# Attention kernel: the weighing of the values by a block's probabilities in one piece, in the first of four steps, in place of two halves two steps apart

## The chip, the cores and the metric

The kernel runs on one core of one Trainium2 chip. The metric is the device time of one execution in microseconds (us). The names of the engines are those of the profile: PE is TensorE's matmul, PEld its loading of weights, DVE is VectorE, ACT is ScalarE, POOL is GpSimd and SP is SyncE, which here issues the DMAs.

## The reference

Two residual layers follow one another on x of shape (4, 32, 32, 384). The first is a selective scan in four directions and is not touched here. The second is attention over the 1024 tokens of an image with 12 heads of 32 channels:

```python
qkv = (x.reshape(B, L, dim) @ w_qkv + b_qkv).reshape(B, L, 3, nh, hd)
q, k = rot(q), rot(k)
attn = jnp.einsum('bnqd,bnkd->bnqk', q, k) * scale
attn = attn.reshape(B, nh, H, W, H, W) + rel_h[..., :, None] + rel_w[..., None, :]
attn = jax.nn.softmax(attn.reshape(B, nh, L, L), axis=-1)
out = jnp.einsum('bnqk,bnkd->bnqd', attn, v)
...
return out @ w_proj + b_proj
```

The change concerns the second einsum, the sum over the keys of probability times value.

## The kernel before

**Stages.** The scan of the four images takes the first 1,700 us or so; nothing of it is touched. Then the four images go through attention one after the other. An image has three groups of four heads (`GROUPS` is 3, `HG` is 4), a group has eight blocks of 128 queries (`QB` is 8). One head of one block is a step: 32 steps in a group (`STEPS`), 96 in an image. Block n of an image has the steps 4n to 4n + 3.

**What is done for a step s.** TensorE makes the scores of 128 queries against 1024 keys (`scores`, line 880, two matmuls of 64 rows by 512 columns). VectorE adds the bias and takes the largest (`biased_scores`, line 1201), ScalarE takes the exponential (line 1526), TensorE turns the 128 by 1024 probabilities in eight transposes (`turn_probs`, line 891), and the turned ones are copied from PSUM to `PT`: by VectorE for even s (line 1155), by ScalarE for odd s (line 1503); both functions are called `save_turned`. When all four heads of a block are turned and saved, TensorE weighs the values with them (`weigh`, line 905): 32 matmuls, eight tiles of keys times four heads, each with 128 rows, 32 output channels and 128 queries. The four heads write into four parts of one PSUM region. ScalarE copies the sum out (`save_sums`, line 1509).

**Order on each engine.** Nothing here is placed by a scheduler: each engine's queue is written out and holds the steps in this order.

- TensorE at step s: `scores(s + 2)`, then a job if the step has one, then a piece of `weigh` if s is odd, then `turn_probs(s)`. `scores(s)` waits until the turned probabilities of step s - 4 are saved, since both use the same PSUM banks. `turn_probs(s)` waits for the exponential of s and for the largest of s + 1.
- VectorE at step s: if s is odd `save_turned(s - 3)`, then `biased_scores(s)`, then its part of a job.
- ScalarE at step s: if s is even `save_turned(s - 3)`, in one step of four `save_sums`, then the exponential of s, then its part of a job.

**Jobs.** A table `JOB_AT` puts other work into some steps. In group 0 nearly every even step has one (k = 2, 4, 6, 8, 10, 12, 16, 18, 20, 22, 24 and 26, and also 25 and 27): first projections of the next groups' q and k (line 561, three matmuls), then products with the tables of relative positions (lines 854 and 843). Group 1 has two projections, at k = 6 and 10. In group 2 the table `LATE_AT` has sums, normalizations and output projections at k = 2, 4, 6, 8, 10, 12, 20, 22, 24, 26 and 28 (lines 925, 934 and 561). All other steps hold attention alone.

**Change of group.** The operands of the next group's head j are brought by six DMAs (line 542), which SP issues once `scores` of step 32g - 4 + j has been done. `scores(32g + j)` waits for them.

**Weighing before.** In each block n but the last of an image, the two calls `weigh(n, 0)` and `weigh(n, 1)`, of 16 matmuls each, stand in steps 4n + 5 and 4n + 7. The last block is weighed in one call behind the loop.

Of the kernel before, what the change touches and what calls it, by code (L numbers as in the profile page):

```python
# [19 lines left out]
HG = P // HD  # L20
# [121 lines left out]
def build(nc, x, mats, cols, sel_in, onehot, b_rows, z_rows, x1, xn2, out):  # L142
    ctx = ExitStack()
    with ctx:
# [30 lines left out]
        def banks(k, n=2):  # L175
            return PS[:, k * HALF:(k + n) * HALF]
# [380 lines left out]
        def _(pe):  # L557
# [222 lines left out]
            for b in range(B):  # L780
                for i in range(ITEMS):
                    s, n = divmod(i, NST)
# [21 lines left out]
            for b in range(B):  # L804
# [58 lines left out]
                def wait_turned_saved(s):  # L863

                    pe.wait_ge(pt_saved[s % 2].sem, pt_saved[s % 2].after(b, s // 2 + 1))

                def scores(s):
                    g, k = divmod(s, STEPS)
                    qb, j = divmod(k, HG)
                    if qb == 0:  # L870
                        pe.wait_ge(head_loaded[j].sem, head_loaded[j].after(b, HEAD_DMAS * (g + 1)))
                    if s == 1:
                        pe.wait_ge(rel_saved.sem, rel_saved.after(b, 2))
                    elif s == 3:
                        pe.wait_ge(max_done.sem, max_done.after(b, 2))
                    elif s >= 4:
                        wait_turned_saved(s - 4)
                    for h in range(2):
                        rows = slice(2 * HD * h, 2 * HD * h + 2 * HD)
                        last = pe.matmul(scores_place(s)[:, h * HALF:(h + 1) * HALF],  # L880
                                         QX[rows, j, qb * P:(qb + 1) * P], KX[rows, j, :], start=True, stop=True)
                    last.then_inc(s_psum.sem, 1)

                def turn_probs(s):
                    pe.wait_ge(exp_done.sem, exp_done.after(b, s + 1))
                    if s + 1 < STEPS * GROUPS:
                        pe.wait_ge(max_done.sem, max_done.after(b, s + 2))
                    else:
                        wait_turned_saved(s - 3)
                    for t in range(QB):  # L890
                        last = pe.transpose(turned_place(s)[:, t * P:(t + 1) * P], PR[s % 3][:, t * P:(t + 1) * P], idn)  # L891
                    last.then_inc(pt_psum.sem, 1)

                def weigh(n, part, parts=2):

                    g = n // QB
                    if part == 0:
                        for s in (HG * n + HG - 2, HG * n + HG - 1):
                            wait_turned_saved(s)
                        if n:  # L900
                            pe.wait_ge(o_saved.sem, o_saved.after(b, n))
                    for t in range(part * QB // parts, (part + 1) * QB // parts):
                        for j in range(HG):
                            head = HG * g + j
                            last = pe.matmul(banks(6, 1)[HD * j:HD * j + HD, (n % 2) * P:(n % 2 + 1) * P],  # L905
                                             V[:, t, head * HD:(head + 1) * HD], PT[:, n % 2, j, t, :],
                                             start=(t == 0), stop=(t == QB - 1), skip_group_check=True)
                    if part == parts - 1:
                        last.then_inc(o_psum.sem, 1)
# [36 lines left out]
                def project(m, ks):  # L946
                    for k in ks:
                        last = pe.matmul(banks(m, 1), W["w_proj"][:, k, m * P:(m + 1) * P], OT[:, k, HALF:L],  # L948
                                         start=(k == 0), stop=(k == CT - 1), skip_group_check=True)
                    return last  # L950
# [11 lines left out]
                for s in range(STEPS * GROUPS):  # L962
                    g, k = divmod(s, STEPS)
                    if s + 2 < STEPS * GROUPS:
                        scores(s + 2)
                    if k in JOB_AT[g]:
                        job(g + 1, JOB_AT[g][k])
                    if g + 1 == GROUPS and k in LATE_AT:
                        late(LATE_AT[k])
                    if s % 2 == 1 and s > HG:  # L970
                        weigh((s - HG - 1) // HG, (s - HG - 1) % HG // 2)
                    if s + 1 == STEPS * GROUPS:
                        wait_turned_saved(s - 2)
                        project(0, (0, 1))
                        project(1, (0, 1))
                    turn_probs(s)
# [793 lines left out]
```

## Time and profile before

| what | value |
|---|---|
| median of 3 runs | 3094.75 us (3092.77 to 3095.74) |
| profiled execution | 3094.16 us |
| its span in the trace | 3092.4 us |
| PE busy | 2684.6 us, 87% of the span |
| DVE busy | 2242.5 us, 73% |
| ACT busy | 1614.7 us, 52% |
| POOL busy | 1351.2 us, 44% |
| mean granted TensorE clock | 0.968 of full speed |

A row of a timeline gives the start in us from the start of the span, the duration of the row, the engine, the line and operation, what it writes and reads, and how many instructions follow one another in it. A float32 matmul has two records, so the two matmuls of `scores` are x4 and 16 matmuls of `weigh` are x32. In brackets stands how long the engine was idle before it and who ended that. The ends of matmuls are modelled, so distances between the starts of two rows are the safer measure of TensorE.

### The profile page before, as it was taken

Reading aid. Unit: us, or ns where it says so; the run is one execution under the profiler, and the core shown is the slowest. Engines: PE = TensorE matmul, PEld = TensorE weight load, DVE = VectorE, ACT = ScalarE, POOL = GpSimd, SP = SyncE. Lnnn points to the kernel's source line nnn. Section 1 sums busy time; section 2 is a strip of 40 time slices with the busy share of each in tenths; the row PEclk is TensorE's granted clock in tenths of the full one; section 3 lists DMA queues with packets and bytes.
Section 4 is the critical chain, followed back from the end, with each engine's and each line's share of the span. In section 5 each row is a group of like instructions: output and inputs, shape, how many; then the busy total and the mean of one; then the engine's idle time right before and its main releaser. Section 6 shows DMA issues by size and latency. Waiting matters only on the chain. (4 is left out here: it accounts for less than half of the span.)

```text
span 3092.4 us, 40835 instructions
## 1 busy us (share of the span) xinstructions
PE 2684.6 (87%) x16088; PEld 1346.6 (44%) x16088; DVE 2242.5 (73%) x2157; ACT 1614.7 (52%) x1972; POOL 1351.2 (44%) x624
## 2 busy tenths in 40 slices
PE   5579788988889878687767999999999999999999
PEld 2134233333333333232322565555555565556555
DVE  0398988899888998899992566646665566646665
ACT  2464655555555556555541456625564356525564
POOL 1577887887778877788670200011000300011000
PEclk9799999999999999999996999999999999999999
DMA  2344544455444555445551210120120210120110
GB/s 78 108 142 129 163 150 144 150 140 168 165 145 148 142 170 167 154 160 140 197 172 36 76 36 18 39 75 1 36 56 14 63 36 22 35 76 1 35 36 22
DMA packets 93526, 297.03 MB, mean 96 GB/s; under 512 B 16172, under 2 KB 18872, under 8 KB 93208
## 3 DMA queue, kind: packets, MB, share of 16 engines
q1 hardware_dynamic: 93336, 294.43, 30.8%
q8 instruction: 128, 2.10, 0.3%
q14 instruction: 62, 0.51, 0.1%
HBM read 238.27 MB, written 23.07 MB: 85 GB/s over the span
## 5 line engine op out<-in xcount | busy, mean ns | idle before, releaser
L1599 POOL TENSOR_TENSOR arena<-arena 128x1024 f32<-128x1024 f32 x384 | 903.2, 2357 | 307.4 <-DVE arena L1081 297.7
L1081 DVE TENSOR_TENSOR_SCAN arena<-PS,arena 128x1024 f32<-128x1024 f32 x384 | 879.0, 2289 | 102.2 <-ACT PS L1442 70.9
L577 PE MATMUL PS<-arena,ident 128*128 128x512 f32 x1536 | 762.0, 620 | 15.0 <-ACT arena L1453 12.8
L1442 ACT ACTIVATE PS<-arena,a_inf,a_neg 128x1024 f32<-128x1024 f32 x384 | 463.8, 1208 | 586.3 <-DVE arena L1081 580.3
L1201 DVE CUSTOM_DVE_ANT_1 arena<-PS,arena 128x1024 f32<-128x1024 f32 x384 | 467.7, 1219 | 323.4 <-PE PS L880 321.8
L1526 ACT ACTIVATE arena<-arena,neg_max 128x1024 f32<-128x1024 f32 x384 | 441.0, 1148 | 494.8 <-DVE neg_max L1201 494.8
L1089 DVE TENSOR_TENSOR arena<-arena,PS 128x1024 f32<-128x1024 f32 x384 | 460.8, 1200 | 57.7 <-PE PS L568 56.4
L568 PE MATMUL PS<-arena,sel 96*128 96x512 bf16 x768 | 239.4, 394 | 295.5 <-DVE arena L1089 291.7
L1629 POOL TENSOR_TENSOR arena<-arena 128x512 f32<-128x512 f32 x48 | 68.4, 1425 | 955.2 <-ACT arena L1495 955.2
L880 PE MATMUL PS<-arena 64*128 64x512 f32 x1536 | 431.6, 640 | 19.3 <-DMA arena<-arena 12.8
L577 PEld LDWEIGHTS PS<-arena,ident 128*128 128x128 f32 x1536 | 302.5, 198 | 275.0 <-issue 221.4
L891 PE MATMUL PS<-ident,arena 128*128 128x128 f32 x3072 | 414.7, 278 | 3.8 <-ACT arena L1526 3.6
L891 PEld LDWEIGHTS PS<-ident,arena 128*128 128x128 f32 x3072 | 334.9, 142 | 154.9 <-issue 92.5
L568 PEld LDWEIGHTS PS<-arena,sel 96*128 96x128 bf16 x768 | 55.9, 100 | 577.5 <-DVE arena L1089 503.3
L1155 DVE COPY arena<-PS 128x1024 f32<-128x1024 f32 x192 | 233.9, 1218 | 60.6 <-PE PS L891 57.2
L905 PEld LDWEIGHTS PS<-arena 128*32 128x32 f32 x6144 | 157.0, 110 | 134.0 <-issue 131.7
L905 PE MATMUL PS<-arena 128*32 128x128 f32 x6144 | 206.5, 276 | 0.0
L1503 ACT ACTIVATE arena<-PS 128x1024 f32<-128x1024 f32 x192 | 192.7, 1004 | 19.4 <-PE PS L891 19.4
L880 PEld LDWEIGHTS PS<-arena 64*128 64x128 f32 x1536 | 116.5, 185 | 88.5 <-issue 59.0
L1636 POOL TENSOR_TENSOR arena<-arena 128x512 f32<-128x512 f32 x48 | 64.0, 1333 | 176.3 <-DVE arena L1126 175.7
L561 PE MATMUL PS<-normed,arena 128*128 128x512 f32 x288 | 135.7, 615 | 0.6 <-DVE g_tmp L1025 0.6
L577 PE MATMUL PS<-arena 128*128 128x512 f32 (+1 forms) x224 | 108.3, 622 | 12.0 <-ACT arena L1305 5.5
(125 smaller groups left out, 2205.3 us busy)
## 6 DMA issues: line engine op xcount, KB each, us to landing
arena<-b_rows SPq DMA_DIRECT2D x256, 512.0 KB, 3.7
arena<-b_rows SPq DMA_DIRECT2D x256, 256.0 KB, 3.9
arena<-arena SPq DMA_DIRECT2D x192, 128.0 KB, 3.3
arena<-arena SPq DMA_DIRECT2D x120, 64.0 KB, 2.6
normed<-x_in SPq DMA_DIRECT2D x12, 512.0 KB, 5.4
residual<-x_in SPq DMA_DIRECT2D x12, 512.0 KB, 5.6
x<-residual SPq DMA_DIRECT2D x12, 512.0 KB, 5.3
xn<-residual SPq DMA_DIRECT2D x12, 512.0 KB, 4.7
```

The source lines that it names most:

```text
L568: last = pe.matmul(dst[:, half(h)], lhs, rhs(h), start=(k == 0), stop=(k == len(pairs) - 1))
L577: last = pe.matmul(dst[:, half(h)], lhs, rhs[:, half(h)], start=start, stop=stop, skip_group_check=True)
L880: last = pe.matmul(scores_place(s)[:, h * HALF:(h + 1) * HALF], QX[rows, j, qb * P:(qb + 1) * P], KX[rows, j, :], start=True, stop=True)
L891: last = pe.transpose(turned_place(s)[:, t * P:(t + 1) * P], PR[s % 3][:, t * P:(t + 1) * P], idn)
L905: last = pe.matmul(banks(6, 1)[HD * j:HD * j + HD, (n % 2) * P:(n % 2 + 1) * P], V[:, t, head * HD:(head + 1) * HD], PT[:, n % 2, j, t, :] ...
L1081: dve.tensor_tensor_scan(HS[:, at % 2, ::step], DA[:, ::step], DBU[:, at % R3, ::step], 0.0, ALU.mult, ALU.add).then_inc(scan_done.sem, 1)
L1089: dve.tensor_tensor(HC[:, at % R_HC, :], HS[:, at % 2, :], C_PSUM, ALU.mult).then_inc(hc_ready.sem, 1)
L1155: dve.tensor_copy(PT[:, n % 2, s % HG, :, :], turned_place(s).rearrange("p (t q) -> p t q", t=QB)).then_inc(pt_saved[0].sem, 1)
L1201: dve.tensor_tensor_reduce(out=PR[s % 3].rearrange("p (h w) -> p h w", w=IMG), in0=scores_place(s).rearrange("p (h w) -> p h w", w=IMG), i ...
L1442: act.activation(DA, DELTA[:, tile % 2, :], ACT.Exp, bias=a_inf[:, col:col + 1], scale=a_neg[:, col:col + 1]).then_inc(da_ready.sem, 1)
L1526: act.activation(PR[s % 3], PR[s % 3], ACT.Exp, bias=neg_max[:, s % 4:s % 4 + 1], scale=-1.0, accum_out=row_sum[:, qb, at:at + 1]).then_in ...
L1599: pool.tensor_tensor(DBU[:, at % R3, :], DU[:, tile % 2, :], BSB[:, at % R3, :], ALU.mult).then_inc(dbu_ready.sem, 1)
```

## The change

`weigh` is called once for a block, in step 4n + 5, with all 32 matmuls. The step 4n + 7 has no piece of it any more. The 32 matmuls and their order within the block are the same, and no other engine's queue changes.

```diff
@@ -967,8 +967,8 @@
                         job(g + 1, JOB_AT[g][k])
                     if g + 1 == GROUPS and k in LATE_AT:
                         late(LATE_AT[k])
-                    if s % 2 == 1 and s > HG:
-                        weigh((s - HG - 1) // HG, (s - HG - 1) % HG // 2)
+                    if s % HG == 1 and s > HG:
+                        weigh(s // HG - 1, 0, 1)
                     if s + 1 == STEPS * GROUPS:
                         wait_turned_saved(s - 2)
                         project(0, (0, 1))
```

TensorE's queue in group 1 behind its last job, before. L880 is `scores`, L905 `weigh`, L891 `turn_probs`; here a matmul counts once.

```order
1165 L880 MATMUL PS<-arena 128x512 x2
1166 L905 MATMUL PS<-arena 32x128 x16
1167 L891 MATMUL PS<-ident,arena 128x128 x8
1168 L880 MATMUL PS<-arena 128x512 x2
1169 L891 MATMUL PS<-ident,arena 128x128 x8
1170 L880 MATMUL PS<-arena 128x512 x2
1171 L905 MATMUL PS<-arena 32x128 x16
1172 L891 MATMUL PS<-ident,arena 128x128 x8
1173 L880 MATMUL PS<-arena 128x512 x2
1174 L891 MATMUL PS<-ident,arena 128x128 x8
```

The same four steps in the changed kernel:

```order
1155 L880 MATMUL PS<-arena 128x512 x2
1156 L905 MATMUL PS<-arena 32x128 x32
1157 L891 MATMUL PS<-ident,arena 128x128 x8
1158 L880 MATMUL PS<-arena 128x512 x2
1159 L891 MATMUL PS<-ident,arena 128x128 x8
1160 L880 MATMUL PS<-arena 128x512 x2
1161 L891 MATMUL PS<-ident,arena 128x128 x8
1162 L880 MATMUL PS<-arena 128x512 x2
1163 L891 MATMUL PS<-ident,arena 128x128 x8
```

Four steps held two pieces of 16 in alternate steps; now one step holds 32, and three steps in a row hold scores and transposes alone.

TensorE's queue at the end of an image, before. L948 is the output projection.

```order
1296 L880 MATMUL PS<-arena 128x512 x2
1297 L905 MATMUL PS<-arena 32x128 x16
1298 L891 MATMUL PS<-ident,arena 128x128 x16
1299 L905 MATMUL PS<-arena 32x128 x16
1300 L948 MATMUL PS<-arena 128x512 x4
1301 L891 MATMUL PS<-ident,arena 128x128 x8
```

And in the changed kernel:

```order
1274 L880 MATMUL PS<-arena 128x512 x2
1275 L905 MATMUL PS<-arena 32x128 x32
1276 L891 MATMUL PS<-ident,arena 128x128 x16
1277 L948 MATMUL PS<-arena 128x512 x4
1278 L891 MATMUL PS<-ident,arena 128x128 x8
```

The 16 matmuls that stood between the transposes and the output projection now stand ahead of the transposes.

## Rows read from the trace of the kernel before

**Rows 1.** The page, busy time, share of the span and instructions of each engine.

```profile
PE 2684.6 (87%) x16088; PEld 1346.6 (44%) x16088; DVE 2242.5 (73%) x2157; ACT 1614.7 (52%) x1972; POOL 1351.2 (44%) x624
```

**Rows 2.** Windows: busy us (instructions) by engine, granted clock, DMA share, GB/s.

```profile
2197.13:2288.60 91.47, 88.36 (x910) 52.42 (x910) 59.23 (x86) 56.47 (x91) 5.09 (x4) 1.00 0.16 34
2083.66:2394.30 310.64, 303.90 (x2992) 180.19 (x2993) 200.28 (x292) 172.01 (x272) 20.13 (x16) 1.00 0.11 27
```

**Rows 3.** Timeline of TensorE over two steps in group 1 without a job.

```profile
2205.40 1.13 PE L880 MATMUL PS<-arena 64*128 64x512 f32 x4
2206.46 1.09 PE L891 MATMUL PS<-ident,arena 128*128 128x128 f32 x8
2207.48 1.13 PE L880 MATMUL PS<-arena 64*128 64x512 f32 x4
2208.54 1.08 PE L905 MATMUL PS<-arena 128*32 128x128 f32 x32
2209.55 1.09 PE L891 MATMUL PS<-ident,arena 128*128 128x128 f32 x8
```

**Rows 4.** Timeline of TensorE where a product of the same shape precedes `weigh`.

```profile
2173.63 1.08 PE L843 MATMUL PS<-arena 128*32 128x128 f32 x32
2174.53 1.06 PE L905 MATMUL PS<-arena 128*32 128x128 f32 x32
2175.52 1.09 PE L891 MATMUL PS<-ident,arena 128*128 128x128 f32 x8
```

**Rows 5.** Timeline of all engines, group 1, from one `scores` on.

```profile
2200.23 1.13 PE L880 MATMUL PS<-arena 64*128 64x512 f32 x4
...
2201.40 1.22 DVE L1201 CUSTOM_DVE_ANT_1 arena<-PS,arena 128x1024 f32<-128x1024 f32 x1 [1.86 <-PE PS L880]
...
2202.55 1.22 DVE L1155 COPY arena<-PS 128x1024 f32<-128x1024 f32 x1
...
2203.69 1.21 DVE L1201 CUSTOM_DVE_ANT_1 arena<-PS,arena 128x1024 f32<-128x1024 f32 x1
...
2204.94 1.15 ACT L1526 ACTIVATE arena<-arena,neg_max 128x1024 f32<-128x1024 f32 x1 [1.03 <-DVE neg_max L1201]
...
2206.09 1.00 ACT L1503 ACTIVATE arena<-PS 128x1024 f32<-128x1024 f32 x1
```

**Rows 6.** Timeline at the one wait in an image of `scores` for ScalarE's copy.

```profile
2238.75 1.00 ACT L1503 ACTIVATE arena<-PS 128x1024 f32<-128x1024 f32 x1
...
2239.81 1.13 PE L880 MATMUL PS<-arena 64*128 64x512 f32 x4 [1.03 <-ACT arena L1503]
```

**Rows 7.** Timeline in group 0, step 16: VectorE's copy and `scores(18)`, which waits for it.

```profile
2140.14 1.22 DVE L1155 COPY arena<-PS 128x1024 f32<-128x1024 f32 x1
...
2141.45 1.13 PE L880 MATMUL PS<-arena 64*128 64x512 f32 x4
```

**Rows 8.** Timeline of SP and TensorE at the two changes of group of one image.

```profile
2177.77 16.00 SPq L542 DMA_DIRECT2D arena<-arena  x24
...
2197.13 1.13 PE L880 MATMUL PS<-arena 64*128 64x512 f32 x4 [1.03 <-DMA arena<-arena]
...
2288.55 1.13 PE L880 MATMUL PS<-arena 64*128 64x512 f32 x4 [0.80 <-DMA arena<-arena]
```

**Rows 9.** Timeline in group 1 with a projection in step 38 (the scores start 1.06 earlier).

```profile
2211.64 2.84 PE L561 MATMUL PS<-normed,arena 128*128 128x512 f32 x6
...
2215.28 1.13 PE L880 MATMUL PS<-arena 64*128 64x512 f32 x4
...
2218.94 1.00 ACT L1503 ACTIVATE arena<-PS 128x1024 f32<-128x1024 f32 x1
```

**Rows 10.** Timeline at the end of an image: ScalarE's copy of step 93, then the projection.

```profile
2032.61 1.00 ACT L1503 ACTIVATE arena<-PS 128x1024 f32<-128x1024 f32 x1
...
2033.93 3.70 PE L948 MATMUL PS<-arena 128*128 128x512 f32 x8
```

## The prediction, made before the changed kernel ran

> **What bounds the kernel now.** I read the page first: TensorE is busy for 87% of the span, VectorE for 73%, ScalarE for 52% [rows 1]. Such shares average over stages, so the second view is the windows over one image of attention: of 310.64 us TensorE is busy for 303.90, VectorE for 200.28, ScalarE for 172.01 [rows 2]. Attention is bound by TensorE with 2% of idle, and the four images do the same, so each term below is worked out for one image and taken four times. What remains to be asked is how much slack the other engines have, since the change leaves TensorE's work alone and only moves it. That is read from the timeline, from start to start.
>
> On TensorE scores take 1.06 us until the transposes start, the transposes 1.02 until the next scores, and a piece of 16 weighing matmuls adds 1.01 (2208.54 to 2209.55) [rows 3]. So a bare step takes 2.08, a step with a piece 3.09.
>
> Beside it runs a chain over the other engines, which starts with `scores(36)` at 2200.23: largest on VectorE at 2201.40, VectorE's copy at 2202.55, the next largest at 2203.69, its exponential on ScalarE at 2204.94, ScalarE's copy at 2206.09 [rows 5]. That copy frees the banks for `scores(39)`. How long after its start the scores can go is seen where they do wait for it: 2238.75 to 2239.81, 1.06 us [rows 6]. So the chain from `scores(36)` until `scores(39)` may start is 2206.09 + 1.06 - 2200.23 = 6.92 us. TensorE needs for the same way (steps 34, 35 and 36: bare, with a piece, bare) 2207.48 - 2200.23 = 7.25 [rows 3, 5]. The slack is 0.33 us: this is the number on which the change turns.
>
> **The change, first part: the block in one piece.** Between `weigh` and the transposes TensorE needs more than between two rows of `weigh`'s own shape: 16 matmuls take 0.90 when 16 of the same shape follow, and 0.99 to 1.01 when the transposes follow [rows 3, 4]. So 32 in a row take 0.90 + 0.99 = 1.89 in place of 2 x 1.01 = 2.02: 0.13 gained a block. Of 23 blocks of an image one gains nothing, that of steps 25 and 27: there a product of the same shape stands ahead of both pieces already (before 2 x 1.89 = 3.78; afterwards 0.90 + 1.89 and 1.01, 3.80). Gain: 22 x 0.13 = 2.86 us an image.
>
> A rule bears on this. The Trainium skill, TensorEngine Tiling (Array Packing), section Key Properties, says that "Changing tiling mode (not just tile) drains the TensorE". The 0.90 against 1.01 agrees. By that rule alone the change removes a pair of mode changes a block and is a gain; that is the first rival below.
>
> **Second part: three bare steps in a row.** The steps 4n + 2, 4n + 3 and 4n + 4 now hold scores and transposes alone, so TensorE comes from `scores(4n + 4)` to `scores(4n + 7)` in 3 x 2.08 = 6.24 us. The chain still takes 6.92; it starts anew at each `scores`, since VectorE was idle for 1.86 before it [rows 5]. TensorE waits 6.92 - 6.24 = **0.68 us**, and the weighing of step 4n + 5 is queued behind the waiting scores. The heavy step cannot give this back: its 32 matmuls come after the wait, and the time that they leave to the others is not needed. The other waits of a bare step hold: VectorE's copy starts 2.32 after `scores(36)` and takes 1.22 [rows 5], so it ends at 3.54, and the scores of an even step that need it start at 4.16. What `weigh` waits for was saved before its scores started, and ScalarE's short `save_sums` is over within the 1.06 of the scores.
>
> There are 22 such places in an image (n = 1 to 22); what differs is what else is in the three steps:
>
> - Five in group 1 (`scores` 39, 51, 55, 59, 63) and one in group 2 (83) are bare: 6 x 0.68 = 4.08.
> - Two in group 1 (43, 47) have a projection in the first of the three steps. It delays the copies as well as TensorE. The chain from the scores at 2210.58 ends at 2218.94 + 1.06 = 2220.00, 9.42; TensorE needs 2215.28 - 2210.58 = 4.70 and two bare steps, 8.86 [rows 9]. Wait 0.56 each: 1.12.
> - Two in group 2 (75, 87) have four short transposes of sums in the last step, which cover part. Between 0 and 0.68 each; I take half, 0.68 for both.
> - Ten have a longer job in the second or third step: six in group 0 (11 to 31) and four in group 2 (71, 79, 91, 95). A projection adds 4.70 - 2.08 = 2.62 [rows 9] and VectorE's part of an earlier one adds less to the chain. Nothing.
> - Two fall on the change of group (35, 67), next.
>
> **Third part: waits that exist already and grow.** (a) `scores(18)` in group 0 starts at 2141.45; VectorE's copy before it, delayed by two operations of a job, runs from 2140.14 to 2141.36 [rows 7], so the scores could start at 2141.42. Step 15 loses its piece, TensorE is there at 2140.44: a wait of 0.98. (b) At the first change of group the path is set by SP, whose 24 DMAs are issued from 2177.77 for 16.00 us, and `scores(35)` waits 1.03 [rows 8]. Whatever TensorE saves in the steps 26 to 32 is waited for: one piece, 1.01. (c) At the second, where it waits 0.80 already [rows 8], it saves 3 x 1.01 - 1.89 = 1.14, of which the wait of `scores(63)` has taken 0.68: 0.46 more. (d) At the end of an image the projection starts at 2033.93 and needs ScalarE's copy of step 93, which allows 2032.61 + 1.06 = 2033.67 [rows 10]. Now the transposes of 93 come 0.88 later, behind 32 matmuls, and the copy goes to about 2033.00 and allows 2034.06, while TensorE is ready at 2033.80: 0.26.
>
> **A wait that goes:** the 1.03 of `scores(49)` [rows 6]. `scores(47)` now waits 0.56 itself and the heavy step 45 follows, so TensorE arrives later than the copy.
>
> **Sum for one image.** Waits: 4.08 + 1.12 + 0.68 + 0.98 + 1.01 + 0.46 + 0.26 - 1.03 = 7.56. Gain: 2.86. Net 4.70, for four images 18.8 us. Against the profiled execution's own time: 3094.16 + 18.8 = 3113.0. The median is 0.6 above that execution, which I leave out: **3113 us**, 0.6% slower. If each length in the chain is off by 0.02, a wait is off by about 0.1, for a dozen waits in four images 5 us; the two half-covered places are good for 2.7 either way. The forecast's own range is 3105 to 3121.
>
> **Rivals.**
>
> 1. *The gain of the block alone, no wait: faster.* The step that decides is the copy on ScalarE; if it came 0.68 us sooner than in the rows, the three bare steps would be free and 4 x 2.86 = 11.4 us would be gained: 3083. For it speaks that ScalarE and VectorE are idle for a third of the image and more [rows 2]. Against it: their idle time lies before the chain starts, not in it; its five parts follow one another within 0.1 us [rows 5].
> 2. *The waits, but no gain.* The 0.90 is measured with another line's matmuls ahead [rows 4]; if 32 of `weigh`'s take 2.02, the sum is 4 x 7.56 = 30.2: 3124.
> 3. *The bare steps do not wait, only the special places do.* Then 0.98 + 1.01 + 1.14 + 0.26 - 1.03 - 2.86 = -0.50 an image, 3092, no change. It needs the same early copy as rival 1, with the change of group still set by SP.
> 4. *The clock falls.* Ten short waits an image could cost granted clock. In the stretch with waits of 1.03 and 0.80 and more the granted clock is 1.00, the 2.4 GHz level [rows 2]. If a bare step of 2.08 ran at 1.2 GHz after each of the 40 waits, it would cost 40 x 2.08 = 83 us: 3196. The Trainium skill, TensorE: Matmul & The Clock Gate, section "A second HAM failure mode: psum-queue depth-cycling", describes such a case, a TensorE that "micro-idles between MM groups" and changes between its clock levels; the waits in this trace do not bear it out.
>
> That the change does nothing is excluded: the order of the queue shows 32 matmuls in one row and a step without them.
>
> **How the numbers follow.** Forecast 0.77; rival 1 0.05, rival 2 0.08, rival 3 0.07, rival 4 0.03. A measurement of this kernel tells about 0.2% (6 us) from no change, so faster means below 3088.6 (rival 1), within it rival 3 and a little of the forecast's lower edge, slower the rest: 0.05, 0.08, 0.87. The range leaves out rivals 1, 3 and 4 (0.15), reaches from somewhat below the forecast's own range to rival 2: 3101 to 3125.
>
> **What would show it.** In the changed kernel's waits, `scores` (line 880) should wait for ScalarE's copy (line 1503) about 10 times an image, some 24 us in all, in place of 4 times and 4.1 us; the rows of `weigh` should read x64 with 1.89 until the transposes; the waits of `scores` for the DMAs should be 1.01 and 0.46 longer; VectorE's and ScalarE's busy times should be the same. If `scores(51)` starts without a wait, the chain is wrong; if 32 matmuls take 2.0, the gain is; if group 0 loses more than 1 us an image, the cover by jobs is.

## The result, and the profile of the changed kernel

The changed kernel takes 3111.76 us (median of 6 runs, 3107.41 to 3113.68), the kernel before 3094.6 us beside it. The ratio is 1.0055, with a 95% interval of 1.0043 to 1.0067: slower by 17 us. Forecast were 3113 us in a range of 3101 to 3125, and slower. The profiled execution took 3110.13 us, 15.97 more than the one before.

The waits of TensorE's matmuls in the attention stage of the changed kernel (engine, line and tile, who ended the wait, us in total, times, longest):

```profile
PE PS L880 <- ACT arena L1503: 20.4, 40, 0.6
PE PS L880 <- DMA arena<-arena: 15.8, 13, 1.9
PE PS L948 <- DVE arena L1172: 6.8, 4, 1.7
PE PS L880 <- DVE arena L1155: 3.6, 4, 0.9
...
PE PS L948 <- ACT arena L1503: 1.0, 4, 0.2
```

There are 40 waits of `scores` for ScalarE's copy, ten in each image, where before there was one of 1.03 [rows 6]. New, too, are four for VectorE's copy (`scores(18)`) and four of the projection at the end of an image. The wait of L948 for L1172 was there before, of the same length. So were waits of `scores` for the DMAs; the line of the kernel before is:

```profile
PE PS L880 <- DMA arena<-arena: 12.8, 12, 1.7
```

They grew by 3.0 us in the four images, where the prediction's 1.01 and 0.46 an image make 5.9. This is the one sign of the prediction that came out at half its size; the cause is in the point on the first change of group below.

The timeline in group 1 of the second image, from one `scores` to the one that waits:

```profile
2243.01 1.13 PE L880 MATMUL PS<-arena 64*128 64x512 f32 x4
2244.07 1.09 PE L891 MATMUL PS<-ident,arena 128*128 128x128 f32 x8
2244.19 1.22 DVE L1201 CUSTOM_DVE_ANT_1 arena<-PS,arena 128x1024 f32<-128x1024 f32 x1 [1.55 <-PE PS L880]
2245.10 1.13 PE L880 MATMUL PS<-arena 64*128 64x512 f32 x4
2245.34 0.08 DVE L1201 DVE_READ_ACCUMULATOR2_ANT neg_max<- 128x1 f32 x1
2245.34 1.22 DVE L1155 COPY arena<-PS 128x1024 f32<-128x1024 f32 x1
...
2246.48 1.21 DVE L1201 CUSTOM_DVE_ANT_1 arena<-PS,arena 128x1024 f32<-128x1024 f32 x1
...
2247.18 1.13 PE L880 MATMUL PS<-arena 64*128 64x512 f32 x4
...
2247.73 1.15 ACT L1526 ACTIVATE arena<-arena,neg_max 128x1024 f32<-128x1024 f32 x1 [1.03 <-DVE neg_max L1201]
2248.24 1.09 PE L891 MATMUL PS<-ident,arena 128*128 128x128 f32 x8
...
2248.88 1.00 ACT L1503 ACTIVATE arena<-PS 128x1024 f32<-128x1024 f32 x1
...
2249.93 1.13 PE L880 MATMUL PS<-arena 64*128 64x512 f32 x4 [0.60 <-ACT arena L1503]
```

This is the chain of [rows 5], with the same distances: from the scores at 2243.01 to the copy's start at 2248.88, and 1.05 later, at 2249.93, the scores go: 6.92 us. TensorE's last transposes started at 2248.24, so it was ready at 2248.24 + 1.02 = 2249.26 and lost 0.67. The row's own figure, 0.60, counts from the modelled end of the transposes.

TensorE over the next four steps:

```profile
2249.93 1.13 PE L880 MATMUL PS<-arena 64*128 64x512 f32 x4 [0.60 <-ACT arena L1503]
2250.99 1.95 PE L905 MATMUL PS<-arena 128*32 128x128 f32 x64
2252.88 1.09 PE L891 MATMUL PS<-ident,arena 128*128 128x128 f32 x8
2253.90 1.13 PE L880 MATMUL PS<-arena 64*128 64x512 f32 x4
...
2260.83 1.13 PE L880 MATMUL PS<-arena 64*128 64x512 f32 x4 [0.61 <-ACT arena L1503]
```

The whole block takes 2252.88 - 2250.99 = 1.89 us, as forecast from [rows 4]. A period of four steps takes 2260.83 - 2249.93 = 10.90; before it was twice 2.08 + 3.09, 10.34. The difference, 0.56, is within 0.02 the wait less the gain of the block, 0.67 - 0.13.

Where the 15.97 us are, by the starts of `scores` (L880), mean of the four images in us:

| from scores to scores | before | changed | difference |
|---|---|---|---|
| 0 to 28 (group 0) | 92.88 | 94.02 | +1.14 |
| 28 to 35 (first change of group) | 20.76 | 20.06 | -0.70 |
| 35 to 60 (group 1) | 71.65 | 74.70 | +3.05 |
| 60 to 67 (second change of group) | 19.79 | 19.65 | -0.14 |
| 67 to 95 (group 2) | 86.73 | 87.09 | +0.37 |

That is 3.72 an image, 14.9 for four. Attention began 0.44 later, and 0.6 lie behind `scores(95)`, in the stretches to the next image or to the end. In three images the stretch in group 1 took 74.30; in the fourth it took 75.91, of which more at the end.

### The profile page after: what moved, and what is told of

It is laid out like the page before. It is cut to its first block and busy times, and to the rows that moved or that the text cites. A ratio compares the mean times of both kernels' runs of the same rounds, so it can differ in the third digit from the quotient of the medians.

```text
span 3108.3 us, 40835 instructions
## 1 busy us (share of the span) xinstructions
PE 2674.9 (86%) x16088; PEld 1350.4 (43%) x16088; DVE 2243.9 (72%) x2157; ACT 1616.2 (52%) x1972; POOL 1352.2 (44%) x624
## 5 line engine op out<-in xcount | busy, mean ns | idle before, releaser
L880 PE MATMUL PS<-arena 64*128 64x512 f32 x1536 | 432.1, 641 | 42.1 <-ACT arena L1503 20.4
L891 PEld LDWEIGHTS PS<-ident,arena 128*128 128x128 f32 x3072 | 334.7, 141 | 200.9 <-issue 170.3
L891 PE MATMUL PS<-ident,arena 128*128 128x128 f32 x3072 | 414.8, 278 | 2.7 <-ACT arena L1526 2.7
L905 PEld LDWEIGHTS PS<-arena 128*32 128x32 f32 x6144 | 163.3, 110 | 70.3 <-issue 51.1
L905 PE MATMUL PS<-arena 128*32 128x128 f32 x6144 | 188.8, 275 | 0.0
L880 PEld LDWEIGHTS PS<-arena 64*128 64x128 f32 x1536 | 116.1, 184 | 114.9 <-issue 53.6
```

## The experiments

The theory: three bare steps in a row take 6.24 us and the chain to ScalarE's copy 6.92, so the scores wait; and the changes of group are set by SP's DMAs. The times of the kernel before lay between 3093.6 and 3094.6 us beside each set of runs.

**ScalarE's copy one place earlier, in the changed kernel.**

```diff
-                    if s % 2 == 0 and s > 3:
-                        save_turned(s - 3)
+                    if s % 2 == 1 and s > 2:
+                        save_turned(s - 2)
...
-                save_turned(STEPS * GROUPS - 3)
                 save_sums(QB * GROUPS - 2)
```

> The changed kernel with one more edit: ScalarE copies the turned probabilities of the odd step s - 2 ahead of the exponential of step s (s odd), in place of those of s - 3 ahead of the exponential of s + 1. The same instructions, one place earlier in ScalarE's queue. My theory (the chain over VectorE and ScalarE's exponential to ScalarE's copy takes 6.92 us where three bare steps take 6.24): the copy can run as soon as the transposes are done, the 10 waits of scores for it in an image (0.60 us each in the changed kernel's trace) vanish, and the time falls by about 4 x 5.0 = 20 us from the changed kernel's to about 3 us below the kernel before (3089 to 3094). Part of what is gained in groups 0 and 1 is waited for again at the change of group: the wait of scores(66) and (67) for the DMAs grows to about 3.8 us an image. Rival 'the waits come from TensorE itself or from PSUM, not from the copy's place in the queue': the time stays at 3108 to 3114, with waits of the same number. Rival 'everything is gained': 4 x 2.86 = 11.4 us below the kernel before plus the 4.1 us of its own waits, 3079.

Measured: 3089.91 us (3086.18 to 3097.81), ratio to before 0.9991 (0.9982 to 0.9999), 22 us less than the changed kernel in medians, 20 by the two ratios to the kernel before. Its waits:

```profile
PE PS L880 <- DMA arena<-arena: 19.9, 13, 1.9
PE PS L948 <- DVE arena L1172: 6.8, 4, 1.7
PE PS L880 <- DVE arena L1155: 3.6, 4, 0.9
```

All 40 waits of scores for ScalarE's copy are gone, with the same instructions on every engine. So the place of the copy in ScalarE's queue, behind the exponential of s + 2, is what the bare steps waited for. Part of the gain was eaten by the DMAs, as expected, though less than expected: all waits for them rose from 15.8 to 19.9 us, and by the rows those of `scores(66)` and `(67)` from 2.4 to 3.0 us an image, where 3.8 was expected.

**The same edit in the kernel before.**

> The kernel before with ScalarE's copy one place earlier, as in the run on the changed kernel, the weighing in two halves. My theory: with halves two steps apart the copy has 0.33 us of slack already, so only the one wait of an image for it (1.03 us, scores(49)) goes: 4 us less than the kernel before (about 3090). Rival 'the early copy is a gain of its own in every step': 10 us or more below.

Measured: 3089.6 us, ratio 0.9987 (0.9978 to 0.9996), 4 us less, as the one wait that goes. The order of ScalarE's queue is worth 20 to 22 us behind three bare steps and 4 us where the pieces alternate.

**The chain made longer, in both kernels.** One more small operation on ScalarE ahead of its copy, which writes a tile that nothing reads any more.

```diff
                     if s % 2 == 0 and s > 3:
+                        act.activation(SEL[:, 0, :], W["ident"][0:3 * 2 * NST, 0, :], ACT.Copy)
                         save_turned(s - 3)
```

> The changed kernel with one small extra ScalarE copy (96 x 128 elements, of a size that took 0.27 us in the trace) in front of each copy of turned probabilities, so the chain is longer by about 0.27 us. My theory: each of the 10 waits of an image in which scores wait for ScalarE's copy grows by 0.27, the time by 4 x 2.6 = 10 us to about 3121. Rival (the waits have another cause): no change, 3111.

> The kernel before with the same small extra ScalarE copy in front of each copy of turned probabilities. My theory: the chain has 0.33 us of slack there, so 0.27 more is nearly hidden; only the one wait for the copy (scores(49)) grows and one or two in group 2 begin: 4 x 0.6 = 2.4 us, about 3097. Rival 'extra ScalarE work costs as much in either kernel': 10 us, 3105.

Measured: 3115.82 us (3115.28 to 3123.04), ratio 1.0075 (1.0062 to 1.0088), in the changed kernel; 3096.58 us, ratio 1.001 (1.0001 to 1.0019), in the kernel before. The changed kernel with the extra operation:

```profile
2255.66 0.29 ACT L1521 ACTIVATE sel<-ident 96x128 bf16<-96x128 f32 x1
2255.86 1.00 ACT L1503 ACTIVATE arena<-PS 128x1024 f32<-128x1024 f32 x1
...
2256.91 1.13 PE L880 MATMUL PS<-arena 64*128 64x512 f32 x4 [0.80 <-ACT arena L1503]
```

The operation delays the copy by 0.20, not 0.27, since the copy starts before its end, and the wait grew from 0.60 to 0.80 by the same 0.20. All waits for the copy grew from 20.4 to 29.2 us. In medians that is 4 us in the changed kernel (6 by the ratios) and 3 us in the one before, between intervals of 3 to 4 us to either side, so the medians alone would not tell the theory from its rival here; the rows do. By the starts of scores, in the images without a fall of the clock, the stretch from 35 to 60 grew from 74.30 to 75.47 us in the changed kernel, six waits by 0.20 each, and in the one before from 71.65 to 71.84, one wait by 0.19. With the halves two steps apart scores waited for ScalarE's copy four times, 4.9 us in all, as often as before; the one or two new waits expected in group 2 did not come.

**One part alone: blocks 7 to 14.** In this and the following kernels the call reads as below, with `SPLIT` the blocks in halves and `SECOND` the whole blocks that stand in their last step.

```diff
-                    if s % 2 == 1 and s > HG:
-                        weigh((s - HG - 1) // HG, (s - HG - 1) % HG // 2)
+                    if s % 2 == 1 and s > HG:
+                        n, part = (s - HG - 1) // HG, (s - HG - 1) % HG // 2
+                        if n in SPLIT:
+                            weigh(n, part)
+                        elif part == (n in SECOND):
+                            weigh(n, 0, 1)
```

> The change made for the eight blocks 7 to 14 of an image alone (steps 33 to 61, in group 1, where few steps have a job); all other blocks are weighed in two halves. My theory: seven waits of scores for ScalarE's copy (five of 0.68, two of 0.56, less the 1.03 that goes) and 0.46 at the second change of group, less 8 x 0.13: 4 x 2.8 = 11 us slower, about 3104. Rival 'the loss is spread evenly over all steps': 8/22 of 17 us, 6 us, 3100.

Measured: 3105.62 us (3101.99 to 3106.2), ratio 1.0035 (1.0023 to 1.0048): 11 us for eight of 22 blocks, the larger part of the loss, where few steps hold a job. Its scores waited for ScalarE's copy 28 times, seven an image as expected.

**The other part: only blocks whose bare steps end with a job.**

> The change made only for the seven blocks 0, 1, 3, 4, 17, 20 and 21 of an image, where a job lies in the last of the three bare steps; all others are weighed in two halves. My theory: no wait is added and each block gains 0.13: 4 x 0.9 = 3.6 us less than the kernel before, about 3090. Rival 'whole blocks cost something wherever they are': 3099.

Measured: 3088.58 us, ratio 0.9985 (0.9976 to 0.9994), 6 us less than before. Whole blocks are a gain where a job gives the chain its time. The waits for ScalarE's copy are the four of the kernel before. By the starts of scores, group 0 takes 92.31 in place of 92.88, 0.57 for four blocks (0.14 each), and group 2 (in three of the four images) 86.31 in place of 86.73, 0.42 for three.

**The whole block in its last step.**

> The whole block is weighed in the last of its four steps (4n + 7) in place of the first. My theory: three bare steps in a row remain, so scores(4n + 9) wait 0.66 for ScalarE's copy in group 1 and elsewhere, and scores(44) and (48) 0.81 for VectorE's, but the wait for the DMAs at the change of group shrinks because two whole blocks lie in its window: 4 x 2.9 = 12 us slower than before, about 3105, less than the change. Rival 'it is the early place of the block that costs': about 3094.

Measured: 3107.81 us, ratio 1.0044 (1.003 to 1.0058). Its waits (the lines of this kernel stand one lower on TensorE and five lower on the others):

```profile
PE PS L881 <- ACT arena L1508: 27.6, 42, 1.0
PE PS L881 <- DVE arena L1160: 7.2, 8, 0.9
...
PE PS L881 <- DMA arena<-arena: 2.4, 3, 1.2
```

It is the three bare steps in a row that cost, not where among the four the block stands. The DMA waits nearly vanish, because two whole blocks lie in the time of SP's DMAs.

**The change of group by itself: two blocks moved.** The changed kernel with blocks 5 and 13 in their last step.

> The changed kernel with one edit: the blocks 5 and 13 of an image are weighed whole in their last step (27 and 59) in place of their first (25 and 57), so that 32 matmuls more lie behind scores(28) and scores(60), that is within the time in which SP issues the 24 DMAs of the next group. ScalarE's queue is as in the changed kernel. My theory (the change of group is set by SP's DMAs, whatever TensorE does meanwhile): the waits for the DMAs shrink by nearly the work moved, 4 x 3 = 12 us less than the changed kernel, about 3099 to 3100. Rival 'the DMAs only follow TensorE': no change, 3111.

Measured: 3100.94 us (3098.66 to 3102.1), ratio to before 1.0023 (1.0014 to 1.0032), 11 us less than the changed kernel:

```profile
PE PS L881 <- ACT arena L1508: 23.1, 45, 0.7
...
PE PS L881 <- DMA arena<-arena: 5.6, 7, 1.5
```

The waits for the DMAs fell from 15.8 to 5.6 us, those for the copy rose by 2.7. Two blocks of 1.89 us, 3.8 us of work an image, now stand behind `scores(28)` and `scores(60)`, and the time fell by 11 / 4 = 2.7 us an image: most of that work is hidden there, not all. At the first change of group the room is used up. `scores(35)` no longer waits for a DMA in any image, and the stretch from `scores(28)` takes 21.00 us in place of 20.06.

**All of it together.** ScalarE's copy one place earlier, whole blocks in the first step, blocks 2, 5 and 13 in the last, 14 and 22 in halves.

> Whole blocks, ScalarE's copy one place earlier, and three blocks (2, 5, 13) in their last step, 14 and 22 in halves. Blocks 5 and 13 put 32 matmuls into the time in which TensorE waits for the DMAs of the next group; block 2 leaves its piece in step 15, where VectorE's copy is late. My theory: no wait for a copy is left, 21 blocks gain 0.13 and the DMA waits shrink by about 1.7 us an image: 4 x 5.3 = 21 us less than the kernel before, about 3072. Rival 'the DMA waits do not shrink': 3082.

Measured: **3073.52 us** (3070.61 to 3077.04), ratio 0.9934 (0.9922 to 0.9947), 21 us less than the kernel before and 38 less than the changed one.

```profile
PE PS L881 <- DMA arena<-arena: 9.0, 9, 1.8
PE PS L949 <- DVE arena L1177: 6.8, 4, 1.7
PE PS L892 <- ACT arena L1531: 3.5, 4, 0.9
PE PS L881 <- ACT arena L1488: 2.3, 4, 0.6
```

No wait of scores for a copy of turned probabilities is left.

## Why the prediction was right, point by point

- *The slack of 0.33 us and the wait of 0.68.* Right. The chain measured 6.92 again, the wait 0.67, at all the places named (`scores` 39, 51, 55, 59, 63 and 83). A row's own figure is 0.07 less than the loss from start to start (0.60 for 0.67), because it counts from the modelled end of the transposes. For the two places behind a projection 0.56 was forecast; their rows say 0.47 and 0.48, that is 0.54 and 0.55.
- *Ten places covered by jobs.* Right: no wait for the copy in group 0, and none at 71, 79, 91 and 95. The two half-covered ones have 0.29 and 0.23 by their rows, 0.36 and 0.30 with the 0.07, where 0.34 each was taken. That half was a guess between two bounds, and its closeness is luck.
- *The gain of the block.* 0.13 forecast, 1.89 against 2.02 measured, and 0.14 a block in the kernel that merged only covered blocks. Rival 2 falls.
- *The places that grow.* `scores(18)` waits 0.90 to 0.91 by its rows, 0.97 with the 0.07, forecast 0.98; the projection at the end 0.24 by its row, forecast 0.26. The wait of `scores(49)` went, as forecast, and `scores(47)` waits instead.
- *The first change of group: the term that was mis-sized.* I took the whole 1.01 that TensorE saves there as waited for, with SP's 24 DMAs at a fixed 16.00 us [rows 8]. But the wait of `scores(35)` grew by only 0.3 on the mean of the four images, and the stretch from `scores(28)` to `scores(35)` fell from 20.76 to 20.06. It was set by SP in both kernels, for `scores(35)` waited for a DMA in all eight images. The stretch has three parts: until SP starts to issue, the 24 issues, and from the last one until the scores go. Their means are 1.23 + 16.70 + 2.83 before and 1.23 + 16.05 + 2.78 changed. So 0.65 of the 0.70 is SP's own time, and that scatters: 17.20, 16.00, 17.54 and 16.06 in the four images before, of which I had read the shortest, and 15.85 to 16.21 in the changed kernel. In the five profiles that have TensorE's work of before in this stretch the 24 took 16.78 on the mean (single ones 15.45 to 17.68), in the three that have that of the changed kernel 16.34 (15.77 to 17.44). Whether the moved work shortens SP's time or this is chance is not shown. The 0.70 are 2.8 us in four images, as much as the sum (18.8) lies above the profiled difference (15.97).
- *The total, where errors cancel.* The four bare places (`scores` 39, 51, 55 and 59), the two behind a projection and the wait that goes make 2.72 + 1.12 - 1.03 = 2.81 for the stretch in group 1, and seven whole blocks in place of 13 halves add 0.10. It grew by 2.65 in three images, not by 2.91. A part of that is that the 1.03 is a row's own figure, while the new waits were forecast from start to start. In the fourth image it grew by 4.26, since the clock fell there, which the sum does not hold. Without that 1.61 the profiled difference would be 14.4 and the sum 4.4 above it, still inside the range. So it is in part luck that the total came as near as it did.
- *Rival 1 (no wait, all gained)* would need an earlier copy. With the earlier copy of the first experiment the time was 3090, not 3083: `scores(18)` still waits for VectorE's copy (3.6 us in all), and a part of the gain is waited for at the DMAs. That is what rival 3 had priced, the early copy with the special places left: 2 us below the kernel before. Measured were 4 us in medians, 3 by the ratio.
- *Rival 3 (no change)* falls for the changed kernel with the 40 waits. *Rival 4 (the clock)* was ruled out too flatly, see the end.

What stays open: why SP's 24 DMAs at the first change of group take between 15.4 and 17.7 us in kernels whose SP queue is the same.

## What to carry to other kernels

A step that is bound by one engine can hide a chain over the others only as long as every stretch of it is long enough: before work is gathered in one step, add up the chain from the release of the first buffer to the reuse of the last and hold it against the *shortest* stretch that the bound engine will then run through, not against the mean. Where such a chain is too long, the order of the short queues beside it is the cheap cure: here a copy one place earlier on ScalarE, with no instruction more or less, was worth 20 to 22 us. And filler work belongs where the bound engine must wait anyway, here behind the scores that start the next group's DMAs, up to the length of that wait.

## What the runs showed of the hardware that I had not expected

Full clock was not kept behind every wait. At the first change of group in the fourth image the scores waited 1.86 us for a DMA, and the rows that follow are longer:

```profile
2901.90 1.47 PE L880 MATMUL PS<-arena 64*128 64x512 f32 x4 [1.86 <-DMA arena<-arena]
2903.30 3.23 PE L905 MATMUL PS<-arena 128*32 128x128 f32 x64
2906.46 1.09 PE L891 MATMUL PS<-ident,arena 128*128 128x128 f32 x8
```

The 32 matmuls took 3.16 us from start to start in place of 1.89. Over that stretch the windows show a granted clock of 0.63, and of 1.00 over the same length from the same scores in the third image, behind a wait of 1.45 (busy us by engine, granted clock, DMA share, GB/s):

```profile
2901.90:2906.46 4.56, 4.56 (x69) 3.07 (x69) 1.23 (x2) 1.24 (x2) 0.00 (x0) 0.63 0.02 5
2551.78:2556.34 4.56, 4.55 (x80) 3.15 (x80) 1.23 (x2) 2.13 (x5) 0.00 (x0) 1.00 0.01 4
```

So TensorE ran for a time at the lower of its two levels, 1.2 GHz, and group 1 of that image became 1.61 us longer (75.91 against 74.30). It also happened in the first experiment, behind a wait of 1.86:

```profile
1938.39:1948.00 9.61, 8.60 (x87) 5.54 (x88) 4.01 (x6) 1.74 (x5) 0.00 (x0) 0.64 0.60 206
```

That profiled execution has four such places and took 3097.81 us, where the median of its kernel is 3089.91. A stretch longer by 1.6 us is also found in two profiles of kernels with halves at that place: group 2 of one image took 88.34 in the kernel before with the extra operation, in place of 86.72, and 87.90 in place of 86.31 where only covered blocks were whole. So the whole block is not needed for it, though nine of the 11 places counted below lie in kernels that have whole blocks around the changes of group, and the profile of the kernel before has none.

The length of the wait does not settle it. In the eleven profiles `scores` waited 49 times for 1.4 us or longer for a DMA. Behind 11 of these waits, of 1.70 to 2.28 us, the granted clock of the next 4.56 us was 0.63 to 0.66; behind the other 38 it was 1.00, and among these are waits of 1.94 and 2.35. What else decides was not tried. The short waits of 0.6 us did not do this: the second image of the changed kernel, with ten of them and a wait of 1.79 for a DMA besides, was granted 1.00 over its whole length. So of rival 4 there remains about 1.6 us behind some of the long waits at the changes of group, and nothing behind the short ones. The Trainium skill, TensorE: Matmul & The Clock Gate, has a section on such changes of clock from idle gaps ("A second HAM failure mode: psum-queue depth-cycling"); of the short gaps here the rows do not bear it out.
